# A sort's stages by halves around its transposes, and the transposed keys copied out by one engine instead of two

## What is computed

```
edge_index = stack([src, dst])
x = layernorm(x + gcn(x))         # norm of degrees, segment_sum over dst, @ W + b, relu
x = layernorm(x + relu(x @ U.T + segment_sum(x[src], dst) @ V.T))
x = layernorm(x + (concat(segment_sum(x[src], dst) / max(deg, 1), x) @ W.T + b))
x = layernorm(x + gated(x))       # per edge: relu, W2, sigmoid gate; mean over src
```

## Time and profile before

| what | value |
|---|---|
| median of 3 runs | 4379.18 us |
| lowest, highest | 4379.1, 4385.17 us |
| the profiled execution | 4377.39 us |
| its span, first to last instruction | 4375.7 us |
| its mean granted TensorE clock | 0.870 |
| TensorE, DVE, ACT busy | 82%, 55%, 39% |
| compare stages of the sort (line 509) on the chain | 9% |
| transposes of the turns (line 1326) on the chain | 1% |

### The profile page before, as it was taken

The page is one execution under the profiler, slowest core; times in us unless marked ns, Lnnn a source line. Parts: engine busy times, 40 slices in busy tenths (PEclk is TensorE's granted clock), DMA queues, the critical chain, the costliest instruction groups (busy, mean ns, idle before and its releaser), DMA issues.

```text
span 4375.7 us, 127467 instructions
## 1 busy us (share of the span) xinstructions
PE 3589.0 (82%) x39375; PEld 2793.3 (64%) x39376; DVE 2414.6 (55%) x6572; ACT 1724.7 (39%) x3798; POOL 1570.6 (36%) x1730
## 2 busy tenths in 40 slices
PE   5784247777777798898996999889999999999886
PEld 2342123333333598897985877777877777878775
DVE  8988879999999702305024434433434343343344
ACT  5773037777777400001002434333333333343332
POOL 2000010000000000000005777777777777777773
PEclk9896579998888899999996979998889888788996
DMA  1000012222222597796962222222222222222222
GB/s 43 3 4 1 19 61 88 88 97 94 88 88 103 194 349 293 276 349 229 343 244 49 57 51 59 56 55 55 56 54 57 54 56 56 54 57 55 56 55 37
DMA packets 186859, 446.38 MB, mean 102 GB/s; under 512 B 52907, under 2 KB 115379, under 8 KB 180271
## 3 DMA queue, kind: packets, MB, share of 16 engines
q1 hardware_dynamic: 133263, 388.80, 25.6%
q0 software_dynamic: 51328, 54.71, 6.1%
q10 hardware_dynamic: 2208, 2.10, 0.2%
HBM read 357.45 MB, written 87.99 MB: 102 GB/s over the span
## 4 chain that ended last, share of the span: by engine, by line
PE 50%; DVE 19%; issue 10%; DMA 9%; POOL 7%; ACT 3%; ACTq 1%; POOLq 1%; DVEq 1%; SPq 0%; PEldq 0%
PE ps L1444 11%; DVE x L509 9%; PE ps L1419 8%; PE ps L1539 8%; PE ps L1529 7%; PE ps L1551 7%; PE ps L1526 6%; POOL x L994 6%; DMA rows<-adjacency 4%; DMA x<-b_table,gidx 4%; DVE rows L707 4%; ACT stage L1193 1%; PE ps L1326 1%; ACT ps L1174 1%; POOLq L988 1%
## 5 line engine op out<-in xcount | busy, mean ns | idle before, releaser
L994 POOL DMA_INDIRECT x<-b_table,gidx x1568 | 1500.1, 957 | 464.0 <-issue 375.7
L1419 PE MATMUL ps<-rows 128*128 128x448 bf16 x2272 | 650.3, 425 | 222.1 <-DVE rows L707 96.6
L1444 PE MATMUL ps<-x,rows 128*128 x22050 | 684.5, 194 | 57.3 <-DVEq L757 29.4
L1444 PEld LDWEIGHTS ps<-x,rows 128*128 128x128 bf16 x22050 | 667.2, 98 | 75.3 <-issue 65.9
L707 DVE TENSOR_SCALAR rows<-iota_c,x 128x448 bf16<-128x448 bf16 x2272 | 711.0, 408 | 2.3 <-PE ps L1419 2.3
L855 DVE TENSOR_TENSOR x<-x,ps 128x256 f32<-128x256 f32 x440 | 185.3, 421 | 945.2 <-ACT x L1260 942.3
L1419 PEld LDWEIGHTS ps<-rows 128*128 128x128 bf16 x2272 | 332.1, 146 | 540.0 <-issue 422.0
L1539 PE MATMUL ps<-w2cat,x 65*128 65x128 f32 x3520 | 575.4, 313 | 0.0
L1529 PEld LDWEIGHTS ps<-ident,x 128*64 128x64 f32 x3520 | 486.9, 157 | 106.6 <-issue 42.9
L1551 PE MATMUL ps<-x 128*128 128x65 f32 x3520 | 503.7, 291 | 49.2 <-DVE x L855 48.4
L1539 PEld LDWEIGHTS ps<-w2cat,x 65*128 65x128 f32 x3520 | 485.0, 214 | 89.2 <-issue 87.7
(11 more groups left out here) (280 smaller groups left out, 2490.3 us busy)
## 6 DMA issues: line engine op xcount, KB each, us to landing
rows<-adjacency SPq DMA_DIRECT2D x150, 800.0 KB, 6.2
rows<-adjacency SPq DMA_DIRECT2D x150, 768.0 KB, 6.0
adjacency<-stage SPq DMA_DIRECT2D x50, 1568.0 KB, 5.1
x<-src_rows SPq DMA_DIRECT2D x440, 128.0 KB
x<-b_table,gidx POOLq DMA_INDIRECT x1568
key_rows<-x ACTq DMA_DIRECT2D x1, 1024.0 KB, 4.1
pair_rows<-x ACTq DMA_DIRECT2D x1, 1024.0 KB, 7.3
pair_rows<-x SPq DMA_DIRECT2D x1, 1024.0 KB, 5.4
```

The costliest lines, as they stand in the source:

```text
L994: e.indirect_dma_start(out=BGT[:, s, j, :], out_offset=None, in_=b_table, in_offset=bass.IndirectOffsetOnAxis(ap=gidx[:, s * G + j:s * G + ...
L1419: e.matmul(psf[:, bass.ds(at_bank, WIN)], hot_src[:, k // HOTS, :, k % HOTS], hot_dst[:, k % HOTS, :], start=False, stop=False, skip_group ...
L1444: ins = e.matmul(acc_ps[:, t, :], rows[:, h, c:c + P], x3[:, bass.ds(2 * pr + h // 2, 1), k * D:(k + 1) * D] .rearrange("p a f -> p (a f)" ...
```

## The change

Around each turn the stage is cut in two at column 1024. The stage ahead of a turn is done for the first 1024 columns, which counts a new semaphore `half_sorted`, and then for the others, which counts `sorted_step`. TensorE transposes eight blocks behind the first and eight behind the second. ACT copies all four banks, in order, and counts `turn_out` for each. DVE copies none. The stage behind the turn is done for the first 1024 columns when two banks are out, and for the others when four are. A turn is no step of `sorted_step` now: `stages[n]` is the number of stages ahead of step n. `SHARES` has ten entries instead of nine with the same sum of 522: four fewer steps ahead of each of the turns 1 to 8, and 32 ahead of turn 9, which had none. The other stages, and all behind the sort, stay.

```diff
--- before
+++ after
@@ -71,7 +71,7 @@
-SHARES = [280, 26, 30, 27, 30, 31, 30, 36, 32]
+SHARES = [280, 22, 26, 23, 26, 27, 26, 32, 28, 32]
...
@@ -469,26 +471,20 @@
 
             n_turn = 0
             for n, s in enumerate(plan):
-                if n:
-                    e.wait_ge(sorted_step, n)
-                if n and plan[n - 1]["kind"] == "turn":
-                    e.wait_ge(turn_out, n_turn)
-                a, b = keys[s["src"]], keys[s["dst"]]
-                if s["kind"] == "sign":
-                    c = s["bit"] - COL_BITS
-                    ins = e.tensor_scalar(b, a, sign[:, c:c + 1], None, ALU.mult)
-                elif s["kind"] == "turn":
-                    for bank in (1, 3):
-                        e.wait_ge(turned, 4 * n_turn + bank + 1)
-                        r = slice(bank * 512, bank * 512 + 512)
-                        if s["bit"] is None:
-                            ins = e.tensor_copy(b[:, r], turn_ps[:, r])
-                        else:
-                            c = s["bit"] - COL_BITS
-                            ins = e.tensor_scalar(b[:, r], turn_ps[:, r], sign[:, c:c + 1], None, ALU.mult)
+                if s["kind"] == "turn":
                     n_turn += 1
-                else:
-                    cj, ck = s["stride"], s["direction"]
+                    continue
+                turned_in = n > 0 and plan[n - 1]["kind"] == "turn"
+                turned_next = n + 1 < last and plan[n + 1]["kind"] == "turn"
+                if n and not turned_in:
+                    e.wait_ge(sorted_step, stages[n])
+                halves = 2 if turned_in or turned_next else 1
+                for half in range(halves):
+                    if turned_in:
+                        e.wait_ge(turn_out, 4 * (n_turn - 1) + 2 * half + 2)
+                    r = slice(half * COLS // halves, (half + 1) * COLS // halves)
+                    a, b = keys[s["src"]][:, r], keys[s["dst"]][:, r]
+                    cj, ck = s.get("stride"), s.get("direction")
 
                     def view(t, high, down):
...
@@ -498,18 +494,24 @@
-                        for high in (0, 1):
-                            op = ALU.min if high == down else ALU.max
-                            if s["unflip"]:
-                                ins = e.scalar_tensor_tensor(out=view(b, high, down), in0=view(a, 1, down),
-                                                             scalar=-1.0, in1=view(a, 0, down),
-                                                             op0=ALU.mult, op1=op)
-                            else:
-                                ins = e.tensor_tensor(view(b, high, down), view(a, 0, down),
-                                                      view(a, 1, down), op)
+                    if s["kind"] == "sign":
+                        c = s["bit"] - COL_BITS
+                        ins = e.tensor_scalar(b, a, sign[:, c:c + 1], None, ALU.mult)
+                    else:
+                        for down in ((0,) if ck is None else (0, 1)):
+                            for high in (0, 1):
+                                op = ALU.min if high == down else ALU.max
+                                if s["unflip"]:
+                                    ins = e.scalar_tensor_tensor(out=view(b, high, down), in0=view(a, 1, down),
+                                                                 scalar=-1.0, in1=view(a, 0, down),
+                                                                 op0=ALU.mult, op1=op)
+                                else:
+                                    ins = e.tensor_tensor(view(b, high, down), view(a, 0, down),
+                                                          view(a, 1, down), op)
+                    if turned_next and half == 0:
+                        ins.then_inc(half_sorted, 1)
                 ins.then_inc(sorted_step, 1)
-            e.wait_ge(sorted_step, last)
+            e.wait_ge(sorted_step, stages[last])
 
 
 
...
@@ -1141,15 +1143,14 @@
                     e.wait_ge(dve, mark["consts_dve"])
-                for bank in (0, 2):
+                c = None if s["bit"] is None else s["bit"] - COL_BITS
+                for bank in range(4):
                     e.wait_ge(turned, 4 * k + bank + 1)
                     r = slice(bank * 512, bank * 512 + 512)
-                    c = None if s["bit"] is None else s["bit"] - COL_BITS
-                    ins = e.activation(keys[s["dst"]][:, r], turn_ps[:, r], ACT.Copy,
-                                       scale=1.0 if c is None else sign[:, c:c + 1])
-                ins.then_inc(turn_out, 1)
-
-            e.wait_ge(sorted_step, last)
+                    e.activation(keys[s["dst"]][:, r], turn_ps[:, r], ACT.Copy,
+                                 scale=1.0 if c is None else sign[:, c:c + 1]).then_inc(turn_out, 1)
+
+            e.wait_ge(sorted_step, stages[last])
             e.dma_start(key_rows.rearrange("(p a) e -> p (a e)", p=P), keys[last % 2]).then_inc(keys_stored, 16)
             e.dma_start(pair_rows.rearrange("(p m) (w e) -> p w m e", p=P, w=2)[:, 0, :, :],
...
@@ -1321,14 +1322,17 @@
-                e.wait_ge(sorted_step, n)
                 for m in range(COLS // P):
+                    if m == 0:
+                        e.wait_ge(half_sorted, k + 1)
+                    if m == COLS // P // 2:
+                        e.wait_ge(sorted_step, stages[n])
                     ins = e.transpose(turn_ps[:, m * P:(m + 1) * P], keys[plan[n]["src"]][:, m * P:(m + 1) * P],
                                       ident[:])
                     if m % 4 == 3:
                         ins.then_inc(turned, 1)
 
-            e.wait_ge(sorted_step, last)
+            e.wait_ge(sorted_step, stages[last])
...
```

More of the change, by code:

```diff
@@ L125, in build_gnn @@
     last = len(plan)
+    stages = [n - sum(t < n for t in turns) for n in range(last + 1)]
     adj = nc.dram_tensor("adjacency", [MTILES * P, MCOLS], BF16).ap()
@@ L321, in build_gnn @@
         sorted_step = sem("sorted_step")
+        half_sorted = sem("half_sorted")
         turned = sem("turned")
@@ L499, in view @@
                         return w[:, :, down, :, high, :] if ck > cj else w[:, :, high, :, down, :]
-                    for down in ((0,) if ck is None else (0, 1)):
-                        for high in (0, 1):
-                            op = ALU.min if high == down else ALU.max
-                            if s["unflip"]:
-                                ins = e.scalar_tensor_tensor(out=view(b, high, down), in0=view(a, 1, down),
-                                                             scalar=-1.0, in1=view(a, 0, down),
-                                                             op0=ALU.mult, op1=op)
-                            else:
-                                ins = e.tensor_tensor(view(b, high, down), view(a, 0, down),
-                                                      view(a, 1, down), op)
+                    if s["kind"] == "sign":
[14 more added lines that the diff above has]
+                        ins.then_inc(half_sorted, 1)
                 ins.then_inc(sorted_step, 1)
-            e.wait_ge(sorted_step, last)
+            e.wait_ge(sorted_step, stages[last])
             S = keys[last % 2]
```

## The result

| | median us | lowest to highest | runs |
|---|---|---|---|
| before, first comparison | 4380.16 | 4379.1 to 4385.17 | 4 |
| changed | 4342.12 | 4338.88 to 4350.17 | 4 |
| before, second comparison | 4377.45 | 4366.81 to 4388.05 | 23 |
| changed | 4353.04 | 4338.94 to 4358.35 | 5 |

The ratio of the changed kernel to the one before is 0.9916 in the first comparison (95% interval 0.9897 to 0.9934) and 0.9946 in the second (0.9931 to 0.9962): 38 and 24 us faster, where 31 were forecast. The kernel is faster, beyond 0.2%. Single runs of the changed kernel lie up to 19 us apart, so the size is read better from the traces, where the sort ends at 499.1 us (497.8 in the second trace) instead of 526.0.

What follows compares the result with a forecast made beforehand. VectorE (DVE) was taken to bound the sort, losing 4.06 us a turn. Slow turns 16.4 plus quick turns 14.5 gave 30.9 us off the 4379.18 us median: 4348.3 us forecast, range 4340 to 4359.

Steps and rivals of the forecast that it cites:

- Slow turns: Seven turns of the sort (0, 3, 9 to 13) with transposes taking 3.67 us: overlap saves 16.4 us in sum.
- Quick turns: The other seven turns, behind the grid matmuls: half 2 starts 2.45 us behind the stage ahead, saving 14.5 us.
- rival A: Clock has fallen in every second half of the quick turns: 2.45 us less gain, 4350.7 us; chance 0.10.
- the part on the grid shares: Grid steps between turns: 0.9 us of room left at turn 1, and the 32 steps ahead of turn 9 hidden.
- Instructions on VectorE: Halved stages of the sort: 80 more instructions at 0.066 us fixed each, 5.3 us of added work.
- Rival B: Each added small instruction in the sort costs its whole 0.150 us: 6.7 us less gain, 4355 us; chance 0.08.
- C: Grid shares ahead of turns come late, steps at 0.66 us: no gain, 4380 us, or half, 4364; chance 0.08.
- D: Sort gains, but the edge loop behind it gets a lower clock, costing about 40 us: 4388 us; chance 0.04.

Runs made afterwards that it cites:

- copy_only: Kernel before with ScalarE copying all four banks, no stage halved, shares as before: 4378.87 us, ratio 1.0009, sort end 527.6 us.
- dve_copies: Changed kernel with its halves and new shares, but VectorE copies banks 1 and 3 again: 4356.75 us, ratio to before 0.9953, sort end 504.9 us.
- old_shares: Changed kernel with the grid shares of before, in the comparison with the slow edge loop: 5212.58 us, ratio to before 0.9941, sort end 492.6 us.
- quarters_shares: Changed kernel with stages cut into four pieces of 512 columns and the grid shares of before: 4328.06 us, ratio to before 0.9899.
- fill_more: Changed kernel with the grid shares of before plus unneeded TensorE products ahead of turns 0 and 9 to 13: 4333.27 us, ratio to before 0.9900.
- old_shares_again: Changed kernel with the grid shares of before, measured once more in a later comparison: 4341.39 us, ratio to before 0.9928, sort end 492.3 us.
- fill: Changed kernel plus unneeded TensorE products of constants ahead of each turn: 5205.18 us, ratio to before 0.9921, sort end 491.5 us.

## Why the prediction was right, and where it was off

**Bound and place.** VectorE's compares bound the sort and the turn cost it 4.06 us on the mean; the gain was to come from overlap, and it did. copy_only and dve_copies show that the overlap is the cause: with the new shares it gives 21 us, and the freed copies give nothing by themselves and 6 us on top of it.

**Slow turns.** Half 2 was put at 3.15 us behind the end of the stage ahead; turn 12 has 3.19. The end of the stage behind was put at 4.40, and is 4.48: half 2 starts 0.04 later and is 1.29 long and not 1.25. The waits of the seven slow turns sum to 12.0 us, forecast were 12.4.

**Quick turns.** This is the term that was mis-sized. I took the middle between clocks, 2.45 us to half 2, and 1.07 us of waits a turn, 7.5 in all; the rows sum to 11.1, for five of the seven began at the lower clock, which neither my middle nor rival A (quick first half, slow second) had; the two that began quick, turns 1 and 4, went as A has it. The prediction says that these turns "come straight behind the grid matmuls". They don't: TensorE stood idle for 2.1 to 3.7 us ahead of each (3.04 at turn 4, in the earlier trace rows), long enough for either start, so that their speed was not safe to carry over. And in the part on the grid shares I looked only at lateness: I worked out 0.9 us of room between ScalarE's last sign and turn 1 (1.4 measured: 224.11 to 225.54) and read room as safety. In the changed kernel TensorE idles 2.0 to 3.6 us ahead of turns 1 to 8; with four more steps each it idles 0 to 1.8, every turn starts quick and the sort ends 6 us earlier (old_shares). That the first trace had only two quick turns, and the second four, is in part luck.

**Instructions on VectorE.** 80 more at 0.066 were 5.3 us. From the sums of before and after, 56.4 us of turns less 23.2 of waits less 26.9 gained leave 6.3. The fixed part was right (0.069 from quarters_shares). The added 1 us lies for the most part at the waits between halves: at turn 12 the two halves read 1.29 us each, 2.58 together, where four instructions in a row took 2.50, and ten of the 14 turns have such a wait, 0.8 us in all. Rival B, the whole 0.150 us each, would have been 12. A stage of 8 x 256 reads 2.77 us, where B wanted over 3.3; this is the one behind turn 2 of the changed kernel:

```profile
246.90 2.77 DVE L505 SCALAR_TENSOR_TENSOR x<-x 128x256 f32<-128x256 f32 x8 [1.49 <-ACT x L1150]
```

The rule of the Trainium skill on the exposed latency ("VectorE: DVE Perf Modes", in the section "The TRN2 errata — SBUF-src ops pay a fixed extra latency per instruction") does not hold here with its figure of about 150 cycles for instructions that stand back to back: start to start they have a fixed part of 0.066 to 0.069 us, even at 128 elements. The length of a single one does fit it: 1222 and 686 ns lie on 0.150 us fixed, and that length is paid in full where a wait stands behind, as between the halves.

**Sum.** 30.9 were forecast and 26.9 came in the first trace, 28.2 in the second: 3.6 of the 4.0 are the waits of the quick turns, and the rest is within the added 1 us of VectorE's instructions. The forecast of 4348.3 lies between the two medians. That the first median was 6 us lower, and not 4 higher, is chance in the stretch behind the sort, and that 4348.3 falls so near the middle of the two is luck.

**The others.** C (late grid shares) did not occur, and even four more steps made no turn late. D would have shown as a longer stretch behind the sort; that was 3849.4 and 3839.5 us long, against 3849.7 before. The 6 us that the prediction allowed for this stretch were too few: two traces of one kernel lie 9.9 us apart.

## What to carry to other kernels

When an engine waits for a transpose or a matmul that takes in its own last result, cut the stages on both sides into pieces that the transposes can follow, and let the copies out be made by an engine that has nothing to compute; the copies alone gave nothing here, and the halves without them 21 of 27 us. Cut finer until the wait is gone, and count the price of an added instruction from start to start in a row of many, not from the length of one. When work is moved away from TensorE to be safe, look at how long it idles ahead of the next burst: behind a pause of some 2 to 4 us the burst started now at the full and now at half the clock here, and the grid steps that had stood there cost nothing.

## What the runs showed of the hardware

TensorE's sixteen transposes of a turn took 2.2 to 2.4 us in most turns behind pauses of 0 to 1.8 us (old_shares, fill_more; the others fell to the lower clock inside, 2.9 to 3.3 us), and 3.5 to 3.7 us behind pauses of about 15 us and more in before and the changed kernel. The granted clock in such stretches is 1.00, the level of 2.4 GHz (turn 6 of old_shares_again, 314.4 to 316.5 us), and 0.50, the level of 1.2 GHz (turn 12 of before, 474.2 to 477.6 us). Behind pauses of 2 to 3.7 us both starts occur: turn 2 began at the lower clock in one trace of the changed kernel and at the higher one in the other, with 2.94 and 2.97 us of idle TensorE ahead of it.

In one of the four comparisons every kernel ran the edge loop about 1.43 times as long as in the others: in fill TensorE did 7647 matmuls between 2450 and 4250 us at a granted clock of 0.70, against 10901 at 0.87 in before. The sort, where VectorE is the bound, took the same time there. This comparison and the last one, in which the kernel before had 4375.84 us, were made on a chip of the same number, so nothing here shows that the chip is the cause; it stays open.
